# A post-norm decoder layer on one core: projections dealt out at the start, bias sums moved, a quarter's integers on POOL

## The reference

```
x = layernorm(x + attention(x))
x = layernorm(x + cross_attention(ctx, x))
def qlinear(x, W, b):
    q, s, z  = round(x / s) + z clipped to -128..127,  s = (max(x) - min(x)) / 255
    wq, sw   = round(W / sw) clipped to -127..127,     sw = max(|W|) / 127
    return ((q - z) @ wq.T) * (s * sw) + b
h = gelu(qlinear(x, W1, b1))          # 128 -> 512
x = layernorm(x + qlinear(h, W2, b2)) # 512 -> 128
```

## Time and profile before

| | us |
|---|---|
| median of 3 runs | 332.87 |
| lowest and highest run | 332.35 and 334.61 |
| own time of the profiled execution | 331.59 |
| its span | 329.9 |
| PE busy | 269.5 (82%) |
| DVE busy | 299.9 (91%) |
| ACT busy | 248.1 (75%) |
| POOL busy | 238.6 (72%) |

### The profile page before, as it was taken

One profiled execution on the slowest core, in us unless ns is written; L12 is line 12 of the kernel. 1 busy time (PEld: TensorE's weight loads), 2 busy tenths in 40 slices (PEclk: granted clock), 3 DMA queues, 4 the chain that ended last, 5 costly groups with the idle time before them and its releaser, 6 DMA issues.

```text
span 329.9 us, 12489 instructions
## 1 busy us (share of the span) xinstructions
PE 269.5 (82%) x4927; PEld 168.4 (51%) x4927; DVE 299.9 (91%) x695; ACT 248.1 (75%) x502; POOL 238.6 (72%) x477
## 2 busy tenths in 40 slices
PE   4677987999999999999999988898887655536991
PEld 3455654666656566665656655555554212112561
DVE  5668799899999999999999999999988779987994
ACT  2237776989988888888888878788775399912995
POOL 2866787897677878687786887776559228998394
PEclk9999999999999999999999999999999897557797
DMA  2353324143342423334243234322100000000025
GB/s 65 111 152 92 108 76 129 52 125 92 107 122 64 123 67 115 84 99 125 69 123 92 79 97 131 90 78 61 52 5 0 3 0 0 1 0 0 2 79 177
DMA packets 48993, 25.14 MB, mean 76 GB/s; under 512 B 6440, under 2 KB 48808, under 8 KB 48936
## 3 DMA queue, kind: packets, MB, share of 16 engines
q1 hardware_dynamic: 46072, 23.55, 24.6%
q10 hardware_dynamic: 2864, 0.80, 1.0%
HBM read 9.39 MB, written 2.10 MB: 35 GB/s over the span
## 4 chain that ended last, share of the span: by engine, by line
POOL 36%; DVE 29%; issue 13%; PE 10%; ACT 5%; SPq 3%; DMA 2%; POOLq 1%; DVEq 0%; ACTq 0%
DVE neg_max L1044 15%; POOL rstd L640 5%; SPq L472 3%; POOL arena_h L670 3%; POOL var_eps L633 2%; ACT arena_h L903 2%; DMA arena_h<-parts_sk 2%; POOL parts_cq L439 2%; POOL parts_ck L439 2%; PE ps L1298 2%; POOL parts_cq L437 2%; POOL parts_ck L437 2%; POOL x_bias L659 2%; DVE o_stats L1206 1%; POOL parts_sq L439 1%
## 5 line engine op out<-in xcount | busy, mean ns | idle before, releaser
L1044 DVE TENSOR_REDUCE neg_max<-ps 128x8 f32<-128x1024 f32 x128 | 156.2, 1220 | 9.5 <-PE ps L1298 9.3
L852 ACT ACTIVATE probs<-ps 128x1024 f32<-128x1024 f32 x64 | 65.5, 1024 | 21.8 <-PE ps L1305 21.8
L843 ACT ACTIVATE probs<-ps 128x1024 f32<-128x1024 f32 x64 | 65.6, 1025 | 15.7 <-PE ps L1305 11.8
L1298 PE MATMUL ps<-arena_h 31*128 31x128 f16 x1024 | 52.3, 220 | 20.4 <-DVE neg_max L1044 11.2
L1298 PEld LDWEIGHTS ps<-arena_h 31*128 31x128 f16 x1024 | 30.5, 94 | 54.9 <-DVE neg_max L1044 38.4
L1305 PE MATMUL ps<-arena_h 32*128 32x128 f16 x1024 | 51.2, 217 | 0.9 <-ACT probs L852 0.9
L1326 PE MATMUL ps<-probs,arena_q 128*32 128x128 f32 x1024 | 41.2, 279 | 1.4 <-ACT u_sb L868 1.4
L1326 PE MATMUL ps<-probs,arena_h 128*32 128x128 f32 x1024 | 41.3, 279 | 0.0
L633 POOL TENSOR_TENSOR var_eps<-mean_var,eps_col 128x1 f32<-128x1 f32 x64 | 12.3, 192 | 38.1 <-DVE mean_var L1026 38.1
L640 POOL TENSOR_TENSOR rstd<-var_eps,minus_half 128x1 f32<-128x1 f32 x64 | 35.3, 551 | 4.7
L1305 PEld LDWEIGHTS ps<-arena_h 32*128 32x128 f16 x1024 | 29.2, 92 | 2.0 <-ACT probs L852 1.5
(11 more groups left out here) (182 smaller groups left out, 657.7 us busy)
## 6 DMA issues: line engine op xcount, KB each, us to landing
arena_h<-parts_sq SPq DMA_DIRECT2D x48, 64.0 KB, 1.9
arena_h<-parts_ck SPq DMA_DIRECT2D x48, 64.0 KB, 2.3
arena_h<-parts_sk SPq DMA_DIRECT2D x46, 64.0 KB, 2.0
arena_h<-parts_cq SPq DMA_DIRECT2D x45, 64.0 KB, 2.2
xT_in<-in_xT_dram SPq DMA_DIRECT2D x16, 128.0 KB, 2.5
xN_in<-in_xN_dram SPq DMA_DIRECT2D x16, 128.0 KB, 2.6
cT_in<-in_cT_dram SPq DMA_DIRECT2D x16, 128.0 KB, 2.5
cN_in<-in_cN_dram SPq DMA_DIRECT2D x16, 128.0 KB, 2.3
```

Source lines behind the costliest of these rows:

```text
L843: act.activation(probs[1][:, :], ps_s2, ACT.Exp, scale=SCALE).then_inc(ex, 1)
L852: act.activation(probs[0][:, :], ps_s2, ACT.Exp, scale=SCALE).then_inc(ex, 1)
L1044: dve.tensor_reduce(neg_max[b.par][:, HH * half:HH * half + HH], ps_s1.rearrange("p (h k) -> p h k", h=HH), AXX, ALU.max, negate=True).the ...
L1298: ins = pe.matmul(ps_s1[:, at:at + S], q[r:r + MAX_AT, j, :], kk[r:r + MAX_AT, j, :], start=True, stop=True, skip_group_check=True)
```

## The change

It has four parts.

**First slots.** x is loaded into four buffers in place of two (`X_LOADS`), the loads of pairs 2 and 3 being issued at once. A table `RAMP` gives each half slot from -2 to 2 at most one projection of the pairs 1 to 4, where a slot had a q and a k projection, or a v projection, in one piece. `q_sums`, `k_sums` and `v_sums` name their places in PSUM; the value sums of pairs 1 and 2 use banks of the second scores, which wait for them. POOL makes the words of q and k of pair 2 and of q of pair 3 earlier, ahead of or behind its block matrices, and `setup_products` stands behind the second scores of slot 0.

**Sums of x2 and the bias.** The words of queries and keys and the ring `x_bias` share one array `arena_x` of the size of x2. The sums go to this array instead of in place, so they need no consumer of x2 to be done, and all four stand right behind POOL's last root. PE reads them from there.

**Folded units.** Five (3, 6, 9, 11, 13) instead of four (3, 6, 9, 12), with an order of reductions on DVE to go with it.

**Integers.** Unit 9's words are made by DVE. The integers of the second quarter (units 4, 6, 5, 7) are made by POOL ahead of its roots, with a semaphore of their own. DVE makes the words of 5, 7 and 9, the integers of the third quarter, and its statistics come in another order.

```diff
-DVE_ALONE = (1, 3, 5, 7)
+DVE_ALONE = (1, 3, 5, 7, 9)
-LOADS = 2
+LOADS, X_LOADS = 2, 4
...
+RAMP = {(-2, 0): ("v", 1), (-2, 1): ("q", 2), (-1, 0): ("k", 2), (-1, 1): ("v", 2), (0, 0): ("q", 3),
+        (1, 0): ("k", 3), (1, 1): ("v", 3), (2, 0): ("q", 4), (2, 1): ("k", 4)}
+RAMP_FIRST, RAMP_LAST = -2, 2
...
-FOLDED_UNITS = (3, 6, 9, 12)
-EXTREMES_ORDER = (1, 2, 4, 5, 3, 7, 8, 6, 10, 11, 9, 13, 14, 12, 15)
+FOLDED_UNITS = (3, 6, 9, 11, 13)
+EXTREMES_ORDER = (1, 2, 4, 5, 3, 7, 8, 6, 10, 12, 9, 14, 11, 15, 13)
...
+        arena_x = sb("arena_x", [128, B * D])
+        x_bias = [arena_x[:, i * 2 * D:(i + 1) * 2 * D].rearrange("p (i d) -> p i d", i=2) for i in range(RING)]
...
@@ POOL, slots
                 i = S_FIRST.get(k + FILL_AT)
-                if i:
+                if i and i != 3:
                     pool.wait_ge(eqk, 2 * i + 2)
                     split(pool, "sk", k_full[:, :], i)
...
-                i = S_FIRST.get(k + QK_AT)
-                if i:
+                i = 3 if k == 0 else S_FIRST.get(k + QK_AT)
+                if i and not (i == 3 and k != 0):
+                    if i == 3:
+                        blocks()
                     pool.wait_ge(eqk, 2 * i + 1)
                     split(pool, "sq", q_full[:, :], i)
...
-                    blocks()
+                if k == 1:
+                    pool.wait_ge(eqk, 2 * 3 + 2)
+                    split(pool, "sk", k_full[:, :], 3)
@@ POOL, feed-forward
             def x2_bias(c):
-                t = x2_all[:, c * 8:(c + 1) * 8, :]
-                pool.tensor_tensor(t, t, b2_wide[:, :].unsqueeze(1).broadcast_to([128, 8, D]),
-                                   ALU.add).then_inc(f_b, 1)
+                if c == B // 8 - 1:
+                    pool.wait_ge(xn, made_to(C_POS[B - 1], False))
+                pool.tensor_tensor(arena_x[:, c * 8 * D:(c + 1) * 8 * D].rearrange("p (b d) -> p b d", d=D),
+                                   x2_all[:, c * 8:(c + 1) * 8, :],
+                                   b2_wide[:, :].unsqueeze(1).broadcast_to([128, 8, D]), ALU.add).then_inc(f_b, 1)
...
+            for c in range(B // 8):
+                x2_bias(c)
             x_ints(2)
             x_ints(3)
             fold_unit(0)
             x_ints(4)
-            fold_unit(1)
-            pool.wait_ge(f_xi, DVE_PIECES)
-            pool.wait_ge(f_xp, NP - DVE_PIECES)
-            x2_bias(0)
-            fold_unit(2)
-            x2_bias(1)
-            fold_unit(3)
-            x2_bias(2)
-            x2_bias(3)
+            for n in range(1, len(FOLDED_UNITS)):
+                fold_unit(n)
...
             out_scale()
+            pool.wait_ge(f_lh, 1)
+            for u in (4, 6, 5, 7):
+                h_ints(u)
@@ DVE, integers and statistics
+            own_words(1)
+            own_words(3)
+            dve.wait_ge(f_lh, 1)
+            for u in INT_ORDER[0:NHC]:
+                h_ints(u)
+            for u in (5, 7, 9):
+                own_words(u)
+            third = INT_ORDER[2 * NHC:3 * NHC]
+            for u in third[0:3]:
+                h_ints(u)
+            o_sums(0)
+            h_ints(third[3])
+            o_sums(1)
+            o_sums(2)
             for half in range(2):
                 for u in INT_ORDER[(NCH - 1) * NHC:]:
                     h_ints(u, half * (CH // 2), CH // 2)
                 if half == 0:
-                    o_sums(NG - 4)
-                    o_sums(NG - 3)
-            o_sums(NG - 2)
-            o_sums(NG - 1)
+                    o_sums(3)
+            for g in range(4, NG):
+                o_sums(g)
@@ PE
                     if s is not None:
+                        if s.pos == 0 and s_half == 0:
+                            pe.wait_ge(evv, 3)
...
+                def ramp(half):
+                    name, i = RAMP.get((k, half), (None, None))
+                    if name == "q":
+                        if i < 4:
+                            pe.wait_ge(eqk, 2 * i - 1)
+                        else:
+                            pe.wait_ge(evv, i)
+                        project_q(i)
+                    if name == "k":
+                        pe.wait_ge(eqk, 2 * i if i < 3 else 2 * i + 1)
+                        project_k(i)
+                    if name == "v":
+                        if i > 2:
+                            pe.wait_ge(eqk, 2 * i + 2)
+                        project_v(i)
...
-                pe.wait_ge(f_hi, (c + 1) * NHC if g < NG - 1 else NU + NHC)
+                if c == 1:
+                    pe.wait_ge(f_hp, NHC)
+                else:
+                    pe.wait_ge(f_hi, (max(c, 1) if g < NG - 1 else NCH) * NHC)
```

More of the change, by code:

```diff
@@ L192, in xT_pairs @@
 def xT_pairs(k):
-    ahead = [(i, XT_AT if i < LEAD_PAIRS else XT_LATER_AT) for i in range(LOADS, PAIRS)]
+    ahead = [(i, XT_AT if i < LEAD_PAIRS else XT_LATER_AT) for i in range(X_LOADS, PAIRS)]
     return [i for i, at in ahead if S_POS[2 * i] - at == k]
@@ L250, in decoder_layer @@
         arena_q = sb("arena_q", [128, NHC * B * S // 2])
-        xT_in = [sb(f"xT_in{i}", [128, PAIR]) for i in range(LOADS)]
+        xT_in = [sb(f"xT_in{i}", [128, PAIR]) for i in range(X_LOADS)]
         cT_in = [sb(f"cT_in{i}", [128, PAIR]) for i in range(LOADS)]
@@ L825, in evacuations @@
[L825 to L832 removed]
+                        v_out(i)
```

175 lines of the change are left out of this document (103 added, 72 removed).

## The result

The kernel after takes 336.88 us (median of 4 runs, 336.38 to 338.1), the kernel before on the same chips 332.94 us (4 runs). The ratio is 1.0121, with a 95% interval from 1.0094 to 1.0147: slower by 3.9 us. The forecast was 337.0. Of all runs in this document one, of the last experiment, took 371.39 us at a granted TensorE clock of 0.661, where its seven others had 0.920 to 0.941; it is left out of the ratio there.

The account below looks back on a forecast made before the run. The wait chain ran 36% through POOL and 29% through DVE, with DVE pacing attention. Terms -2.0 + 4.6 - 2.4 + 3.9 = +4.1 us on the 332.87 median gave 337.0 us, range 331.5 to 339.5.

Parts of the forecast that it names:

- First slots, -2.0: First attention slots: fewer projections ahead of scores and earlier key copies bring DVE's maxima sooner, -2.0 us (bounds 0 and -3.3).
- The maximum of task 5: First slots: this DVE maximum was to come near 32.1 instead of 34.11.
- DVE is the pace at 3.5 us a slot, so the lead is kept: Attention slots after the first ones: DVE sets the pace, so the -2.0 us lasts to the end of attention.
- Sums behind the last root, +4.6: After POOL's last root: four sums hold DVE's last x2, diagonal and x2 integers; gelu stage 4.6 us later (bounds 2.0, 5.4).
- the mechanism of a rival: Behind the last root: the scale's two instructions with two SBUF inputs wait for sums too, gelu 5.4 late; 337.8 us, chance 0.18.
- Folds, -2.4: Feed-forward stage: DVE's waits of 0.80 and 1.02 go, a fifth fold saves 1.04, 0.6 stays; -2.4 us (bounds -2.9, -1.3).
- The end, +3.9: Last stage: POOL's four integer instructions and the new order of statistics delay the last normalisation by 3.9 us (bounds -0.3, +4.2).
- the collision term: End: each of POOL's four integer instructions holds DVE's words and integers 1.15 us; DVE's last statistics end 2.9 us later.
- the roots' row: End: last four statistics groups come every 1.08 us, POOL needs 1.54 per root; last root another 1.0 us late.
- the ports hardly matter: Rival, sums and end: only a DVE instruction already waiting is held, so only the last x2 is late; 330.2 us, chance 0.15.
- POOL's integers don't collide: Rival, end: the sums collide, but POOL's integers may fall beside statistics that read PSUM; 332.8 us, chance 0.17.
- the slots behind task 5 do not keep the lead: Attention slots: stated condition under which the forecast would be wrong; no size given.

Follow-up runs that it names:

- the last experiment: Kernel after with DVE making all integers, two sums cut short behind the last root, two beside the units, and memsets waiting for DVE's x: 330.03 us, ratio 0.9928.
- twelve runs: Kernel before with only the four input buffers and the projections dealt out over the first half slots: 332.00 us, ratio 0.9971.
- the short sums: Kernel after with each of the four sums behind the last root cut into four instructions: 333.55 us, ratio 1.0022.
- the second variant with memsets: Kernel after with the four sums replaced by seven memsets, POOL pausing for a semaphore ahead of each: 336.05 us, one run, not to be compared with the others.
- The experiment with the sums alone: Kernel before with the new first slots and the four sums behind the last root; four folds, DVE makes all integers: 334.99 us, ratio 1.0056.
- The experiments on the order of the statistics: Kernel after, POOL's integers kept: statistics dealt out as before, 335.88 us, ratio 1.0092; only the first group's moved ahead of the third quarter's integers, 335.93 us, ratio 1.0094.

## Why the prediction was right

**First slots, -2.0: the size was wrong, -0.57 in the trace and 1.0 us by twelve runs.** Two steps failed. The maximum of task 5 was to stand 2.0 us sooner and stood 1.12 sooner. The 0.6 us for one projection less came at task 2 (0.57) but was gone again at task 3, since the next two maxima had 0.71 and 0.91 us of idle time ahead of them in place of 0.51 and 0.50; and between the two maxima of task 4 another 0.4 us went, most of it at a 2x2 TENSOR_SCALAR that took 0.67 us in place of 0.34 beside POOL's instruction at 30.54. The second step is "DVE is the pace at 3.5 us a slot, so the lead is kept". The lead in after first grew to 1.8 us at task 11, near what was forecast, and then fell to 0.74 at task 15 and 0.56 at the last. Most of the fall, 0.8 us (1.56 to 0.74), is at the memsets of 66.70, where DVE's instruction took 2.45 us and in before 1.71. The other such place, 43.32 (2.12 us, in before 1.36), cost no lead. Where the clock fell, more went, as shown above.

**Sums behind the last root, +4.6: +5.14, and by the mechanism of a rival.** The x2 lost 2.0 as forecast. The rest was forecast as 0.4 at the diagonal and 2.2 at the integers; of the 3.1 us measured, 0.3 are at the diagonal, 1.1 and 1.5 at the two instructions with two inputs, and 0.3 in longer waits for PE. With these late, the integers started 0.4 us behind the last sum and had nothing to wait for. (The forecast's 4.6 was for the end of these integers; taken there the difference is 5.0.) That a held instruction waits for what is left of POOL's is shown by the short sums; that one with two inputs is held beside a sum and not beside a memset rests on the rows of after and on one instruction of the second variant with memsets.

**Folds, -2.4: -2.15,** with the 0.6 us ahead of the last fold exactly where it was forecast. The forecast's own terms, 0.80 + 1.02 + 1.04 - 0.6, make 2.26 and not 2.4, which is nearer still. The experiment with the sums alone splits it.

**The end, +3.9: +2.4, the collision term over-sized.** That "each POOL instruction holds it for 1.15 us" made 4.6 us for four. The six words and integers of DVE ahead of the first statistics take 6.6 us with 3.5 of their own (3 x 0.70 and 3 x 0.48), so 3.0 us were lost; POOL's instructions were stretched in exchange. DVE's last statistics ended 1.3 us later against the last extreme, and not 2.9. PE's third group did wait for POOL, 2.16 us. The second step, the roots' row with 1.0 us, measured 1.07 (the wait for the last root went from 0.99 to 2.06). But the row of roots is back to back from the first one on, and not only over the last four groups. The experiments on the order of the statistics show that the two steps are not additive: in both that put the first group's statistics ahead part of the loss comes back, and in the old order, 1.5 of the 2.4 us, with POOL's integers still in place. The forecast had put three quarters of this term on the integers alone.

**The rivals.** That the ports hardly matter and that POOL's integers don't collide are out by the rows of after. The condition "if the slots behind task 5 do not keep the lead" was met, and the time was near only because the end cost less by as much. That part of the hit is luck. The measured terms, -0.6 + 5.1 - 2.2 + 2.4 = +4.7, would have made 337.6 on the same footing; the median lies 0.7 below that, since the traced execution of before was 1.3 below its median and that of after 0.5.

## What to carry to other kernels

Before work is moved onto idle GpSimd time, list what VectorE does beside it: here TENSOR_SCALARs from and to SBUF of more than one element a partition, and instructions with two SBUF inputs while GpSimd reads, waited for the rest of the GpSimd instruction, so idle time of GpSimd beside a chain of small VectorE steps is not free. If it has to be there, cut it short (four times shorter instructions took the cost from 5.1 to 1.4 us here), or put it beside reductions. And when a stage ends in a row of equal steps on one engine, time the start of the first one, not the end of the engine that feeds it.

## What the runs showed of the hardware

- Between memsets that GpSimd has queued without a pause, VectorE is passed over at some boundaries and not at others: 3.54 us through two of 1.80; at the five memsets of the fourth ring 2.45 us through all of them in four traces, but 1.70 or 1.71, through the first two, in three others, before among them. With a semaphore wait of GpSimd ahead of each, it was let in after one (1.79). Between the sums it was let in (2.35 and 0.74 us), except for an instruction that came less than 0.1 us before a sum's end (2.40).
- A TENSOR_SCALAR of one element a partition was not held by sums or memsets (0.14, 0.15), one of 2 x 2 elements was (1.79, 2.40).
- Between two engines that both make TENSOR_SCALARs of 1024 elements, both lose: GpSimd 1.63 for 1.19, VectorE 1.52 for 0.70.
- PE's granted clock from 58 to 66 us was 0.79 or 0.86, with a stretch at 0.50, in six traces with the same first slots, and 1.00 in seven. Between tasks 11 and 12 the six lost 1.40 to 1.69 us of lead and the seven 0.12 to 0.38.
